# Weight subtractions moved from GpSimd to VectorE in a one-core transformer layer, save half of each head pair's tile

## The reference, cut to what matters

```
x = x + cross_attention(layernorm(x), ctx, wq, wk, wv, wo)       # one head of width 512, keys: 4096 context rows and 256 own
x = x + latent_attention(layernorm(x), Wqa, Wqb, Wkva, Wkvb, Wo) # 16 heads, 128 + 64 rope columns, causal
x = x + moe(layernorm(x), router, gate, up, down, shared)        # 32 experts of width 256, 8 per token, and a shared one

# moe
scores  = sigmoid(x @ router_w)
# best 4 of 8 groups by the sum of their two best scores (+ bias) are masked to 0; top 8 of the rest
routed  = sum over the 8 chosen e of 2.5 * w_e * (silu(x @ gate_e) * (x @ up_e)) @ down_e
shared  = (silu(x @ sw_gate) * (x @ sw_up)) @ sw_down
```

## Time and profile before

| | us |
|---|---|
| median of 3 runs | 595.43 (595.04 to 597.21) |
| span of the profiled execution, first to last instruction | 593.1 |
| around the span (difference to the median) | 2.3 |
| TensorE busy | 547.3 (92%) |
| VectorE busy | 398.0 (67%) |
| ScalarE busy | 302.7 (51%) |
| GpSimd busy | 205.7 (35%), of it line 270: 195.2 in 73 instructions |
| mean granted TensorE clock | 0.985 |

### The profile page before, as it was taken

How to read it: one execution, slowest core, us unless ns; L and a number is a source line. 1 busy time by engine, 2 the same in 40 slices (tenths; PEclk the granted TensorE clock), 3 DMA queues, 4 the chain that set the end, 5 groups by cost and what they waited for, 6 DMA issues and landing times.

```text
span 593.1 us, 9796 instructions
## 1 busy us (share of the span) xinstructions
PE 547.3 (92%) x3448; PEld 485.4 (82%) x3448; DVE 398.0 (67%) x530; ACT 302.7 (51%) x474; POOL 205.7 (35%) x95
## 2 busy tenths in 40 slices
PE   3999999997789999969969999999999999999997
PEld 3988878885579988849968889888898888988886
DVE  5444443447865566684877787877878778787785
ACT  4555586643256555553616545465454554535531
POOL 1444333343454543521413143232332323323230
PEclk9999999999799999998979999999999999999999
DMA  7565535454222232335324536455364453544620
GB/s 274 164 204 185 170 105 169 151 167 127 80 71 73 81 133 81 106 108 169 117 92 156 178 141 212 134 184 188 130 212 141 177 197 127 207 151 167 203 72 36
DMA packets 19315, 86.57 MB, mean 146 GB/s; under 512 B 2144, under 2 KB 2272, under 8 KB 19296
## 3 DMA queue, kind: packets, MB, share of 16 engines
q1 hardware_dynamic: 19296, 86.32, 43.3%
HBM read 85.79 MB, written 0.52 MB: 146 GB/s over the span
## 4 chain that ended last, share of the span: by engine, by line
PE 57%; DVE 23%; ACT 10%; issue 7%; DMA 1%; POOL 0%; ACTq 0%; SPq 0%; DVEq 0%; POOLq 0%
PE bank L368 19%; PE bank L371 17%; PE bank L372 17%; DVE operands L1410 15%; ACT w_hi L263 6%; ACT operands L1021 3%; PE bank L630 1%; PE bank L477 1%; DVE xn L1056 1%; DMA raw<-wq_dram 1%; DVE scores L1161 1%; DVE operands L281 1%; ACT scores L933 1%; PE bank L613 1%; DVE weights L1400 1%
## 5 line engine op out<-in xcount | busy, mean ns | idle before, releaser
L270 POOL TENSOR_TENSOR w_lo<-raw,w_hi 128x1024 fp32r<-128x1024 f32 (+1 forms) x73 | 195.2, 2675 | 335.9 <-ACT w_hi L263 335.9
L263 ACT CAST w_hi<-raw 128x1280 fp32r<-128x1280 f32 (+2 forms) x162 | 163.7, 1045 | 155.6 <-PE bank L368 140.8
L368 PE MATMUL bank<-xt_hi,w_hi 128*128 128x256 f32 x544 | 156.1, 287 | 7.6 <-DVE w_lo L270 4.8
L371 PE MATMUL bank<-xt_lo,w_hi 128*128 128x256 f32 x544 | 155.6, 286 | 0.0
L372 PE MATMUL bank<-xt_hi,w_lo 128*128 128x256 f32 x544 | 155.4, 286 | 0.0
L368 PE MATMUL bank<-w_hi,operands 128*128 128x512 f32 (+2 forms) x328 | 133.2, 406 | 14.0 <-DVE operands L1410 11.8
L371 PE MATMUL bank<-w_lo,operands 128*128 128x512 f32 (+2 forms) x328 | 129.2, 394 | 0.0
L372 PE MATMUL bank<-w_hi,operands 128*128 128x512 f32 (+2 forms) x328 | 128.2, 391 | 0.0
L1410 DVE TENSOR_TENSOR operands<-scores,operands 128x512 fp32r<-128x512 f32 x32 | 90.1, 2814 | 41.5 <-ACT operands L1021 41.5
L368 PEld LDWEIGHTS bank<-xt_hi,w_hi 128*128 128x128 f32 x544 | 105.4, 194 | 9.7 <-DVE w_lo L270 5.0
L371 PEld LDWEIGHTS bank<-xt_lo,w_hi 128*128 128x128 f32 x544 | 105.4, 194 | 1.3
(11 more groups left out here) (139 smaller groups left out, 528.2 us busy)
## 6 DMA issues: line engine op xcount, KB each, us to landing
raw<-w_exp_dram SPq DMA_DIRECT2D x34, 896.0 KB, 4.8
raw<-w_exp_dram SPq DMA_DIRECT2D x34, 640.0 KB, 5.7
raw<-ctx_t_dram SPq DMA_DIRECT2D x16, 512.0 KB, 3.6
raw<-ctx_n_dram SPq DMA_DIRECT2D x16, 512.0 KB, 3.6
raw<-w_mla_dram SPq DMA_DIRECT2D x16, 512.0 KB, 4.0
raw<-wq_dram SPq DMA_DIRECT2D x2, 512.0 KB, 5.9
raw<-wk_dram SPq DMA_DIRECT2D x2, 512.0 KB, 8.6
raw<-wv_dram SPq DMA_DIRECT2D x2, 512.0 KB, 3.9
```

The lines of the kernel that those rows point to most:

```text
L263: act.copy(w_hi[:, t.slot, at:at + n], raw[:, t.slot, at:at + n]).then_inc(hi_split[k], 1)
L270: eng.tensor_tensor(w_lo[:, t.slot, at:at + n], raw[:, t.slot, at:at + n], w_hi[:, t.slot, at:at + n].bitcast(F32), ALU.subtract) \
L368: ins = pe.matmul(o, a[0], b[0], start=start, stop=False)
L371: pe.matmul(o, a[0], b[1], start=False, stop=False)
```

## The change

All subtractions of weights go from GpSimd to VectorE but those of the second half of each head pair's tile (the output projection), and the rope sums go with them. Three things follow in VectorE's order: the routing starts after three expert splits and the first two residual additions, which stood behind it; after the last pair the first part of expert 1 is split ahead of its third part; and the last pairs' steps are taken out of the loop to have the expert's size. GpSimd keeps the roots and eight splits.

```diff
@@ vector: cross-attention @@
             split_lo(dve, Tile(0, T_WQ), 1, X_SIZES)
-            split_lo(dve, Tile(0, T_WK), 0, X_SIZES)
+            for k in range(2):
+                split_lo(dve, Tile(0, T_WK), k, X_SIZES)
...
-                    split_lo(dve, Tile(j, T_CT + s + 1), 0, X_SIZES)
+                    for k in range(2):
+                        split_lo(dve, Tile(j, T_CT + s + 1), k, X_SIZES)
...
@@ vector: latent attention @@
+            def rope_sum(j, s):
+                at = bass.ds(j * 2 * P + s * P, P)
+                dve.tensor_tensor(q_rope, q_cos[:, :, at], q_sin[:, :, at], ALU.add).then_inc(rope_ready, 1)
...
             tokens_lo(dve, 2, V_OT + 2, ot_hi, ot_lo, 1)
+            split_lo(dve, Tile(0, T_QKV), 1, Q_SIZES)
             add_to_residual(4, F45["wo"], 0, 1)
...
             normalize(1, 4)
+            split_lo(dve, Tile(0, T_ROPE), 0, X_SIZES)
             mean_squares(0, midway=lambda: tokens_lo(dve, 4, V_LN2 + 2, xt_hi, xt_lo, 1))
...
             compressed_rows(0, 5)
+            split_lo(dve, Tile(0, T_ROPE), 1, X_SIZES)
             mean_squares(1)
...
             compressed_kv_lo(1)
+            split_lo(dve, Tile(0, T_M), 0, M_SIZES)
             rope_products(0, 0)
             rope_products(0, 1)
             rope_products(1, 0)
+            dve.wait_ge(rope_part, 9)
+            rope_sum(0, 0)
             rope_products(1, 1)
+            split_lo(dve, Tile(0, T_M + 1), 0, M_SIZES)
...
-            def pair_step(j, s):
+            def pair_step(j, s, sizes=M_SIZES, rope=True):
                 pair_bias(j, s)
+                split_lo(dve, Tile(j, T_M + s + 2), 0, sizes)
                 pair_normalize(j, s)
...
                 pair_rope_v_lo(n + 4, s + 1)
+                if rope:
+                    rope_sum(j, s + 2)
                 out_lo(dve, 5, n + 6, flat(mo_hi[:, :, :]), flat(mo_lo[:, :, :]), 512)
@@ vector: experts @@
             normalize(0, 7)
-            split_lo(dve, Tile(0, T_E + 1), 2, E_SIZES)
+            split_lo(dve, Tile(0, T_E + 1), 0, E_SIZES)
...
             rows_hidden(1, 1)
+            split_lo(dve, Tile(0, T_E + 2), 0, E_SIZES)
             out_lo(dve, 0, V_H, h_hi[:, 0, :], h_lo[:, 0, :], 512)
...
             dve.tensor_copy(score, bank[7][:, 0:2 * E]).then_inc(score_taken, 1)
+            for k in (0, 2):
+                split_lo(dve, Tile(0, T_E + 3), k, E_SIZES)
+            split_lo(dve, Tile(0, T_E + 2), 1, E_SIZES)
+            expert_add(0, 0)
...
-            expert_add(0, 0)
-            split_lo(dve, Tile(0, T_E + 3), 2, E_SIZES)
             expert_add(0, 1)
-            dve.wait_ge(lo_split[1], T_E + 3)
             with dve.Fori(1, NE // 2 - 1) as j:
                 for s in range(2):
                     expert_hidden(j, s)
                     split_lo(dve, Tile(j, T_E + s + 1), 1, E_SIZES)
-                    split_lo(dve, Tile(j, T_E + s + 2), 2, E_SIZES)
+                    for k in (0, 2):
+                        split_lo(dve, Tile(j, T_E + s + 2), k, E_SIZES)
                     expert_add(j, s)
@@ gpsimd: all splits and rope sums taken out; what is left @@
+            for n, at, cols in ((3, 0, 1), (4, 1, 1), (5, 2, 2), (6, 4, 2)):
+                root(n, at, cols)
+            split_lo(pool, Tile(0, T_M), 1, M_SIZES, handed_over=True)
+            with pool.Fori(0, (PAIRS - 2) // 2) as j:
+                for s in range(1, 3):
+                    split_lo(pool, Tile(j, T_M + s), 1, M_SIZES)
+            split_lo(pool, Tile(0, T_M + PAIRS - 1), 1, M_SIZES)
+            for h in range(2):
+                root(7 + h, h, 1)
```

More of the change, by code:

```diff
@@ L1102, in _ @@
             dve.tensor_scalar(exp_bias[:, :], neg_max[:, :], XSCALE, None, ALU.mult).then_inc(bias_ready, 1)
-            split_lo(dve, Tile(0, T_CN), 0, X_SIZES)
+            for k in range(2):
+                split_lo(dve, Tile(0, T_CN), k, X_SIZES)
             for b in range(2):
@@ L1317, in _ @@
             normalize(1, 8)
+            split_lo(dve, Tile(0, T_E + 1), 2, E_SIZES)
+            tokens_lo(dve, 0, V_LN3 + 2, xt_hi, xt_lo, 1)
             split_lo(dve, Tile(0, T_E), 1, E_SIZES, handed_over=True)
-            tokens_lo(dve, 0, V_LN3 + 2, xt_hi, xt_lo, 1)
             def rows_hidden(s, h):
@@ L1353, in by2, with expert_add @@
                 return v[:, 0:32].rearrange("p (g n) -> p g n", n=2)
+            def expert_add(j, s):
+                for h in range(2):
+                    b = 4 + 2 * (s % 2) + h
+                    first = {4: F4, 5: F5, 6: F6, 7: F7}[b]["moe"]
+                    dve.wait_ge(bank_full[b], j + (first + s // 2))
+                    dve.wait_ge(res_done, j * 4 + (3 + 2 * s + h))
+                    w = weights[:, h, bass.ds(j * 2 + s, 1)]
+                    dve.scalar_tensor_tensor(out=res[:, h, :], in0=bank[b][:, :], scalar=w, in1=res[:, h, :],
+                                             op0=ALU.mult, op1=ALU.add).then_inc(res_done, 1)
             dve.wait_ge(bank_full[7], F7["score"])
             dve.tensor_copy(score, bank[7][:, 0:2 * E]).then_inc(score_taken, 1)
+            for k in (0, 2):
+                split_lo(dve, Tile(0, T_E + 3), k, E_SIZES)
+            split_lo(dve, Tile(0, T_E + 2), 1, E_SIZES)
+            expert_add(0, 0)
             dve.wait_ge(score_taken, 1)
@@ L1411, in expert_hidden @@
                                   ALU.subtract).then_inc(ev_lo, 1)
-            def expert_add(j, s):
-                for h in range(2):
-                    b = 4 + 2 * (s % 2) + h
-                    first = {4: F4, 5: F5, 6: F6, 7: F7}[b]["moe"]
-                    dve.wait_ge(bank_full[b], j + (first + s // 2))
-                    dve.wait_ge(res_done, j * 4 + (3 + 2 * s + h))
-                    w = weights[:, h, bass.ds(j * 2 + s, 1)]
-                    dve.scalar_tensor_tensor(out=res[:, h, :], in0=bank[b][:, :], scalar=w, in1=res[:, h, :],
-                                             op0=ALU.mult, op1=ALU.add).then_inc(res_done, 1)
-            expert_add(0, 0)
-            split_lo(dve, Tile(0, T_E + 3), 2, E_SIZES)
             expert_add(0, 1)
-            dve.wait_ge(lo_split[1], T_E + 3)
             with dve.Fori(1, NE // 2 - 1) as j:
```

62 lines of the change are left out of this document (10 added, 52 removed).

## The result

The changed kernel takes 561.62 us (median of 4 runs, 560.89 to 562.30). The kernel before, run beside it, takes 595.23 (594.78 to 597.21). The ratio is 0.942, with a 95% interval of 0.940 to 0.945. The forecast was 562.6. The profiled span fell from 593.1 to 559.1 us, by 34.0 us; the sum of the prediction had 32.8.

A forecast was written before the change was run, and what follows sets the result against it. The prediction held that GpSimd's SBUF reads stop VectorE, so TensorE waits. Gains of 19.1 + 6.8 + 2.3 + 2.9 + 1.7 = 32.8 us take 595.4 to 562.6; own range 557 to 567.5, with three cases 556 to 572.

The forecast's parts named there:

- What bounds the kernel: Whole kernel: TensorE is released late because VectorE is stopped while GpSimd reads SBUF; h_lo takes 3.04 us, shortest 0.69.
- E: Expert loop: 29 stalled experts each gain 0.66 us, 19.1 us in all, bounds 15 to 19.6.
- the first rival: Expert loop: loads become the bound, needing 178 GB/s; experts settle at 8.85 us, total 571; chance 0.09.
- D: Routing, score's copy to second gate_up: blocked small instructions come free, less added splits and additions; gain 6.8 us, bounds 5.0 to 7.4.
- C: After the last head pair: second normalisation no longer blocked, shared expert starts earlier; gain 2.3 us, bounds 1.3 to 3.1.
- B: Head pairs: normalisations no longer meet GpSimd, TensorE's 2.4 us idle is the ceiling; gain 1.7 us, bounds 0 to 2.5.
- A: 137 to 167 us, before the head pairs: 6.3 us blocked against 5.9 added to VectorE; gain 2.9, bounds 0.4 to 5.0.
- Context stages: 30 to 77 us: TensorE has no gap, VectorE's added 1.14 us per tile is hidden; gain zero.
- the slower side: Rival: long times are the instructions' own, not blocks; h_lo stays 3.04 us and the kernel takes 603; chance 0.03.
- serial lower bounds: Rival: in serial stretches VectorE or a kept GpSimd split holds TensorE; gain 25.8 us, total 569.6; chance 0.14.

The follow-up runs named there:

- spare subtraction: Changed kernel plus a 1280-column GpSimd subtraction in the expert loop, on SBUF data nobody uses or waits for: 586.3 us, ratio 0.984.
- spare write: Changed kernel plus, in the expert loop, a one-column GpSimd subtraction and a 4096-column memset that nobody waits for: 567.6 us, ratio 0.954.
- the kernel with the loop's part alone: Kernel before, with only the 30 expert-loop 1280-column splits moved from GpSimd to VectorE: 573.5 us, ratio 0.961.
- the two routing splits given back: Changed kernel, with expert 3's 1280-column and expert 2's 1024-column split back on GpSimd, a 768-column one behind the routing: 562.1 us, ratio 0.942.
- the first halves back: Changed kernel, with first-half splits of head pairs 2 to 7 and of the first expert tile back on GpSimd: 562.6 us, ratio 0.945.

## Why the prediction was right, and where it was not

The forecast of 562.6 stands against 561.6, and the mechanism that carries two thirds of it is shown. Its smaller terms are less good:

- **What bounds the kernel**: shown. The spare subtraction alone brings the time back and the spare write leaves h_lo short, so TensorE waited because VectorE was stopped by GpSimd's reads. All 32 h_lo are at 0.69 and the experts 8.54 apart for 8.55: as written.
- **E** (19.1): 19.9. The 0.66 an expert that the sum took, a little under the difference, was 0.68. The loads kept up at 179 GB/s, the figure that the first rival asked for, and TensorE had no wait for them. The 1280 split lasts 1485 ns, next to the 1.49 us that I estimate from the formula of the Trainium skill (VectorE: DVE Perf Modes, the errata section); the 3.49 us of three splits are 0.08 over my 1.40 + 1.14 + 0.87.
- **D** (6.8, and 12.9 us from copy to product): 6.5 and 12.8, TensorE's wait 0.7 for 0.6. The sum is right. What it is made of the text had only half: 2.6 of the 7.7 us are due to the loop's first split (the kernel with the loop's part alone), and the two others cost 3.0, not 4.95, in the changed order (the two routing splits given back).
- **C** (2.3): 2.6. xn is at 0.55; the slow clock of the stretch went as well, 1.00 for 0.93.
- **B** (1.7, bounds 0 to 2.5): 3.3, outside the bounds. The step that failed is "TensorE idles 2.4 us in 77; that is the ceiling". Busy time of the matmuls was the wrong measure. In 60 us of pairs of the kernel before (180 to 240), the weight loads waited 4.4 us for the normalisation and for a low copy (us in all, times, longest), while the matmul rows show 59.8 of 60 us busy:

```profile
PEld bank L630 <- DVE scores L1236: 2.4, 5, 0.5
PEld bank L368 <- DVE operands L281: 2.0, 5, 0.4
```

  Start to start, a pair took 11.66 us and takes 11.04. Some 4.8 us were to be had: 3.3 measured and 1.5 that the slower clock took in this profile (67.2 for 65.7). Of these, 1.2 came behind the seventh pair's scores (14.5 us to the bias before, 13.3 now). The 1.7 was a choice below a ceiling that was none.
- **A** (2.9, bounds 0.4 to 5.0): 1.6. The blocked time of 6.3 us in it is a slip: its own terms give 2.03 + 2 x 2.05 = 6.1, and the lower bound is 0.2 less. But the miss has another cause. I had laid the four splits into waits by hand; the one of pair 1 has none (it runs 162.64 to 163.86, and the low copies that TensorE waits 2.0 us for start at 163.77). With it moved the stretch takes 26.6 us instead of 27.6 to 28.3, 1.0 to 1.7 us less.
- **Context stages** (0): zero, by the kernel that undoes them.
- **Luck in the sum**: A fell 1.3 us short and B was 1.6 over. That the sum is within 1.2 us owes something to this.
- **Rivals**: the loads as the bound and the slower side did not come. Of the serial lower bounds only the block of VectorE by a kept split was there (1.93 us at the last bias), and the forecast had counted it.

## What to carry over

Before work is spread over VectorE and GpSimd, look for VectorE instructions with two SBUF inputs, or tensor_scalar on SBUF, that are longer than their shortest like (here 3.04 beside 0.69 us), and for a GpSimd instruction that ends when they do or shortly before. Such pairs can be parted by moving the work, by its order (here the instructions that read PSUM ran free), or by 0.7 us of time. Where the loads follow one another in one queue, moving a split later can delay the loads behind it. And what a stage can gain is not read from the busy time of the matmuls: the waits of the weight loads count as well, and the start-to-start distance of its repeats shows what was gained.

## What the runs showed of the hardware

- A write-only GpSimd instruction stopped a tensor_scalar of 32 columns (3.69 us instead of 0.24) and those of 256 (3.45 us for four instead of 1.01), and no tensor_tensor (h_lo 0.69, splits 1.21). Behind a memset the instruction ends with it (292.90 and 292.86); behind a read h_lo ended 0.55 later, near its own 0.69.
- The block works both ways: 0.19 us of GpSimd became 1.25 beside a VectorE split.
- One blocked instruction of 0.24 us on the serial chain cost 6.0 us: 3.5 of its own, and 2.5 in the stretch behind it, where the clock was 0.90.
- In kernels with the same work there, the granted clock of the first pairs differed between executions: six pairs took 65.6 to 68.8 us. With the first halves back, one run had a mean clock of 0.996 and 559.8 us, the five others 0.990 to 0.991 and 562.4 to 563.7. Differences under 3 us between these kernels are read from landmarks and not from the time, and landmarks that span these pairs hold the clock as well.
